# Gated delta rule, chunk stage: norms by ScalarE and TensorE, query rows four steps behind, offset products first

## The reference

```python
def _l2norm(x, eps=1e-06):
    return x * jax.lax.rsqrt(jnp.sum(x * x, axis=-1, keepdims=True) + eps)

def _gated_delta_rule(q, k, v, g, beta):
    q = _l2norm(q) * SCALE
    k = _l2norm(k)
    ...
    def step(S, inp):
        q_t, k_t, v_t, g_t, b_t = inp
        S = S * jnp.exp(g_t)[..., None, None]
        mem = jnp.einsum('bhk,bhkv->bhv', k_t, S)
        delta = (v_t - mem) * b_t[..., None]
        S = S + jnp.einsum('bhk,bhv->bhkv', k_t, delta)
        o_t = jnp.einsum('bhk,bhkv->bhv', q_t, S)
        return (S, o_t)
```

## Time and profile before

| | us |
|---|---|
| median of 3 runs | 886.2 (884.87 to 888.82) |
| the profiled execution | 885.32 |
| its span, first to last instruction | 883.2 |

### The profile page before, as it was taken

How to read it: one execution, slowest core, us unless ns; L and a number is a source line. 1 busy time by engine, 2 the same in 40 slices (tenths; PEclk the granted TensorE clock), 3 DMA queues, 4 the chain that set the end, 5 groups by cost and what they waited for, 6 DMA issues and landing times.

```text
span 883.2 us, 11650 instructions
## 1 busy us (share of the span) xinstructions
PE 787.4 (89%) x4040; PEld 566.3 (64%) x4040; DVE 542.7 (61%) x1302; ACT 252.3 (29%) x402; POOL 210.1 (24%) x191
## 2 busy tenths in 40 slices
PE   5889999888999999998988499799885999999974
PEld 4322333576777777776446478578652899999963
DVE  4599993654444444446799998995478244333426
ACT  2456667332333343333540001221310100000000
POOL 3550000021222222220031000474001344444310
PEclk9989999987999999999999699899997999999995
DMA  9683000101111111140221003400011899999944
GB/s 297 167 195 74 2 3 5 51 19 36 36 53 36 53 36 53 36 144 1 84 96 36 0 1 92 122 1 1 1 48 34 319 340 342 336 350 344 341 138 155
DMA packets 38034, 98.85 MB, mean 112 GB/s; under 512 B 5262, under 2 KB 18118, under 8 KB 37030
## 3 DMA queue, kind: packets, MB, share of 16 engines
q1 hardware_dynamic: 33894, 87.91, 31.1%
q0 software_dynamic: 3648, 9.97, 3.1%
q10 hardware_dynamic: 448, 0.39, 0.2%
HBM read 85.35 MB, written 13.69 MB: 112 GB/s over the span
## 4 chain that ended last, share of the span: by engine, by line
PE 63%; DVE 28%; DMA 4%; ACT 2%; issue 2%; SPq 1%; POOL 0%; ACTq 0%; DVEq 0%; POOLq 0%
PE psum L1246 16%; PE psum L1513 9%; PE psum L1523 8%; PE psum L1257 7%; PE psum L1146 3%; DVE arena L2003 3%; PE psum L1135 3%; PE psum L1125 3%; DVE arena L2062 3%; DVE arena L2055 2%; DVE small L1674 2%; DVE arena L1915 2%; PE psum L1407 1%; PE psum L1325 1%; PE psum L1264 1%
## 5 line engine op out<-in xcount | busy, mean ns | idle before, releaser
L1246 PE MATMUL psum<-xr,wr 128*128 128x512 f32 x600 | 158.8, 415 | 1.1 <-DVE arena L1823 1.1
L1246 PEld LDWEIGHTS psum<-xr,wr 128*128 128x128 f32 x600 | 115.9, 194 | 25.4 <-issue 1.3
L666 POOL TENSOR_TENSOR wr<-ring,wr 128x512 fp32r<-128x512 f32 (+1 forms) x50 | 54.3, 1104 | 197.8 <-ACT wr L829 197.8
L1674 DVE TENSOR_REDUCE small<-psum 128x1 f32<-128x512 f32 x128 | 80.9, 684 | 9.2 <-PE psum L1125 8.5
L1513 PEld LDWEIGHTS psum<-arena 128*128 128x128 f32 x700 | 83.4, 191 | 3.4 <-issue 1.5
L1513 PE MATMUL psum<-arena 128*128 128x128 f32 x700 | 83.9, 274 | 1.1 <-ACT arena L1013 1.1
L1523 PE MATMUL psum<-arena 128*128 128x256 f32 x350 | 81.8, 379 | 1.9 <-DVE arena L2227 1.9
L2216 DVE TENSOR_SCALAR arena<-psum,arena 128x256 f32<-128x256 f32 x35 | 16.9, 484 | 101.4 <-PE psum L1523 101.4
L1786 DVE TENSOR_TENSOR hid<-hid,psum 128x512 f32<-128x512 f32 x50 | 34.4, 688 | 68.4 <-ACT hid L835 68.4
L1257 PE MATMUL psum<-hr,wr 128*128 128x512 f32 x300 | 76.1, 389 | 0.2 <-DVE hr L1761 0.2
L808 ACT ACTIVATE arena<-psum 128x1024 f32<-128x1024 f32 x64 | 63.0, 1023 | 27.1 <-PE psum L1135 26.3
(11 more groups left out here) (360 smaller groups left out, 1232.2 us busy)
## 6 DMA issues: line engine op xcount, KB each, us to landing
arena<-in_w1u SPq DMA_DIRECT2D x35, 642.5 KB
arena<-in_w1d SPq DMA_DIRECT2D x35, 640.0 KB
ring<-in_w SPq DMA_DIRECT2D x25, 384.0 KB, 3.0
part_scratch<-arena SPq DMA_DIRECT2D x12, 256.0 KB, 4.2
arena<-z_scratch SPq DMA_DIRECT2D x8, 384.0 KB, 6.5
arena<-part_scratch SPq DMA_DIRECT2D x9, 256.0 KB, 7.8
qkv_scratch<-arena SPq DMA_DIRECT2D x4, 512.0 KB, 2.8
arena<-qkv_scratch SPq DMA_DIRECT2D x4, 512.0 KB, 4.0
```

Source lines behind the costliest of these rows:

```text
L666: pool.tensor_tensor(wr0[:, k, LO, part], ring0[:, k, part], wr0[:, k, HI, part], ALU.subtract).then_inc(s["w0_lo"], 1)
L1246: ins = pe.matmul(bank[2 * b + m][:, :], wr0[:, k, w, lo:lo + P], xr[:, x, f, half(b)], start=(f == 0 and (w, x) == PARTS[0]), stop=(f == ...
L1674: dve.tensor_reduce(nm[:, g % 2, at16:at16 + 1], full("scores", n), AX, ALU.max, negate=True).then_inc(s["bank_free"], 1)
```

## The change

It is a rewrite of the stage's order on all engines, with the buffers laid out anew to allow it:

- ACT squares k and q (`root`), PE sums the squares with 8 identity matmuls each (`norm_sum`), ACT takes the root from PSUM. The POOL squares and the DVE sums are gone.
- The scaling of the keys and of the queries moves from POOL to DVE. POOL keeps the decays.
- The 12 matmuls that spread the modulation rows go from behind the v convolution to ahead of the layer's projections, in place of a row of 10 warming matmuls; their ACT copies go along.
- PE sums the key pairs ahead of the second half of the v convolution.
- The solve handles the queries four steps behind the keys; the last four query steps stand alone, with the `Xt` rows written between them.
- Query products come first after the solve. The offset product of a key dimension (16 columns) is split from the matrix product (8 columns) and runs three dimensions ahead. All eight output products come last.
- SP turns half of the queries ahead of the offsets, and the rest behind.
- PE sums units 6, 7 and 8, then gathers groups 2 and 3, each in one piece; before, group 2 stood between unit 6 and 7 and group 3 was gathered in two halves.

```diff
+            root(0, k2, "k_to")
             act.wait_ge(s["d_in"], 5)
             act.activation(g_(5), g_(5), ACT.Exp, scale=-1.0).then_inc(s["d_act"], 1)
-            for n in range(2):
-                act.wait_ge(s["d_in"], n + 6)
-                act.activation(g_(8 + n), g_(8 + n), ACT.Sqrt, bias=1e-6).then_inc(s["d_act"], 1)
...
+            root(1, q2, "q_to")
...
+            def norm_sum(n):
...
+                for d in range(DK):
+                    ins = pe.matmul(bank[n][:, 0:CT], ident[:, :], squares(n)[:, d * CT:(d + 1) * CT],
+                                    start=(d == 0), stop=(d == DK - 1))
+                ins.then_inc(s["pair_sum"], 1)
...
             for i in range(C - 1, 0, -1):
-                due = queried(i - 1)
+                p = i + 4 if i < C - 4 else 0
...
+            for k in range(3):
+                offset_product(k)
+            for k in range(DK):
...
+                if k + 3 < DK:
+                    offset_product(k + 3)
...
-                if u in (2, 4, 6):
+                if u in (2, 4):
                     pe.wait_ge(s["state_out"], u)
-                    gather(u // 2 - 1, 0, CC)
-                if u == 7:
-                    pe.wait_ge(s["state_out"], 7)
-                    gather(NCG - 1, 0, 8)
+                    gather(u // 2 - 1)
+            gather(2)
             pe.wait_ge(s["state_out"], len(UNITS))
-            gather(NCG - 1, 8, CC)
+            gather(3)
```

More of the change, by code:

```diff
@@ L581, in _ @@
                              n_dram.rearrange("(h g) (u x) -> u h g x", g=NCG, u=VG)[v]).then_inc(s["n_to"], 16)
[L582 to L589, removed]
+            queries_out((2, 3), "qB_rest")
             for i in range(0, NT, 2):
@@ L679, in _ @@
             ch.link(pool.memset(Di, 1.0))
[L681 to L684, removed]
+            pool.wait_ge(s["d_act"], 7)
             for i in range(1, C):
@@ L890, in _ @@
             norm_out(2)
+            act.wait_ge(s["mod_mm"], 4)
+            for n in range(3):
+                act.activation(rows_mod[:, 4 * n:4 * n + 4, :], bank[4 + n].rearrange("p (m d) -> p m d", d=P),
+                               ACT.Copy).then_inc(s["g_silu"], 1)
             act.wait_ge(s["pads"], 1)
@@ L932, in _ @@
                     ins.then_inc(s["conv_silu"], 1)
+            for n in range(B):
+                conv_silu_v(n)
             for n in range(2 * B):
@@ L935, in _ @@
                 act.activation(yT[:, n // B, half(n % B)], bank[2 + n][:, :], ACT.Silu).then_inc(s["g_silu"], 1)
[L936 to L945, removed]
+            for n in range(B, 2 * B):
+                conv_silu_v(n)
             for x in range(2):
-                act.wait_ge(s["n_sum"], DK + x + 1)
+                act.wait_ge(s["n_sum"], x + 1)
                 act.activation(Qp.rearrange("p (x c t) -> p t x c", x=DK, c=CC)[:, 4 * x:4 * x + 4],
@@ L1307, in _ @@
             back(1)
-            for b in range(B):
-                warm(10, 7)
-                norm_tr(2, b)
+            pe.wait_ge(s["ones"], 5)
+            for m in range(12):
+                ins = pe.matmul(bank[4 + m // 4][:, tile(m % 4)], rows_col[:, m, :], ident[:, :],
+                                start=True, stop=True)
+            ins.then_inc(s["mod_mm"], 1)
+            norm_tr(2, 0)
+            warm(10, 7)
+            norm_tr(2, 1)
             pe.wait_ge(s["ld_sel"], 64)
@@ L1974, in _, with key_group @@
+            def key_group(x):
+                return slice(C + 4 * x, C + 4 * x + 4)
+            solved = [max(l_hi, ends)] * 2
+            asked = 0
             for i in range(C - 1, 0, -1):
-                due = queried(i - 1)
+                p = i + 4 if i < C - 4 else 0
                 prods = []
-                groups = [(slice(C, C + 4), 0), (slice(C + 4, 2 * C), 512), (slice(i, C), 1024)]
-                for x, (part, lo) in enumerate(groups):
+                if p:
+                    asked = max(asked, queried(p))
+                for x in range(2):
@@ L1987, in _ @@
+            ch.need(max(x_rows, asked, *solved))
             dve.memset(Sall[:, 0:VV * DK], 0.0).then_inc(s["blocks"], 1)
```

319 lines of the change are left out of this document (175 added, 144 removed).

## The result

The changed kernel takes **877.9 us**, the median of 4 runs (877.17 to 878.09). The kernel before took 887.5 in the runs made beside it (4 runs, 884.87 to 889.15). The ratio is 0.9875, with a 95% interval of 0.9846 to 0.9904 (it is estimated apart from the medians, whose quotient is 0.9892): faster, by 1.0 to 1.5%. The forecast was 876.0, in a range of 870 to 881.5, so it held. In a later series of five rounds the same kernel gave 877.22 against 888.03, ratio 0.9899 (0.9852 to 0.9945).

The account below looks back on a forecast made before the run. Three terms bound it: DVE to the solve's end (-3.7), what ends last before the scan's first sum (-2.2), PE behind the scan (-4.1). Together -10.0 from 885.3 gives 875.3, with 0.9 for the median 876.0 us; range 870 to 881.5.

Parts of the forecast that it names:

- The decays: POOL's seven small decay instructions fall beside DVE's multiplies, each holding one up for its own length: +2.2 us.
- the norms: DVE's sums over squares move to PE, so the reciprocal of the key norms comes earlier: -4.9 us.
- the cold PE: After the solve, idle PE restarts at a low clock; DVE waits 2.9 us for the first offset sum.
- Ahead of the norms: Spreading matmuls replace warming while DVE normalises; taken as 0, at most +0.5 us.
- POOL's two scalings: Leaving POOL, they no longer stretch two DVE pair multiplies: -4.2 us.
- rival 1: Cheaper than forecast: decays slip between DVE's multiplies (-2.2) or PE is not late (-2.9); down to 871 us, chance 0.15.
- The solve's bubbles: Eight or so steps of the last four query rows depend on their forerunner, 0.13 us each: +0.9 us.
- The turning: Turned offsets, ready 54.6 us after the solve's end, stay hidden before the scan, by 1.0 us only.
- rival 2: Ahead of the scan, the turning or PE stays last: 881 us, chance 0.13.
- The tail: Behind the scan, PE loses one row of gathers (3.6 us) and a 0.5 us wait: -4.1 us.
- Rival 3: Behind the scan, unit 8 waits for POOL and DVE, so 4.1 us does not come: 880 us, chance 0.08.
- Rival 4: PE's clock stays low over the scan's start, the scan waits 7 us, the end takes 14 more: 896 us, chance 0.03.

Follow-up runs that it names:

- e2_pool_scales: Changed kernel with the key and query scalings back on POOL; from layer 1's first DVE scaling to the solve's end 84.47 us instead of 82.42.
- e7_query_beside: Changed kernel with queries solved beside the keys again, Xt rows behind; from layer 1's first DVE scaling to the solve's end 86.21 us, 3.8 more.
- e4_warm_pe: Changed kernel with 54 dummy matmuls on PE during DVE's solve; from the solve's end to the scan's first sum 53.65 us instead of 56.64.
- e5_turn_late: Changed kernel with offsets sent to DRAM only once the block matrices are done; solve's end to scan's first sum 56.98 us instead of 56.64.
- e1_tail_old: Changed kernel with the old order of gathers put back; scan's first sum to the first transpose behind the scan 69.92 us instead of 65.20.
- e8_before_tail_new: Kernel before with only the new order of gathers; scan's first sum to the first transpose behind the scan 65.38 us, 3.9 shorter.
- e3_decays_early: Changed kernel with ACT's exponential for the decays ahead of the key root; layer 1's first DVE scaling to the solve's end 81.59 us, 0.83 less.

## Why the forecast held, step by step

The total of the changed part was forecast at -10.0 and came at -10.1, but that closeness is luck: terms that were off cancelled. The decays were 1.4 cheaper, the norms 0.5 dearer and the stretch behind the solve 1.0 dearer, most of it by the cold PE.

- **Ahead of the norms (0, measured 0).** The spreading matmuls take 2.84 us, and PE's projections end 35.8 us behind g in both kernels.
- **The norms (-4.9, measured -4.4).** The mechanism held: PE's projections ended, the norm sum stood next, and DVE waited for ACT. The path was mis-sized by 0.5 us: PE's 16 instructions took 1.95 instead of 1.8, and from their end to the reciprocal, by way of ACT's root, it took 0.88, where I had allowed 0.55. The squares cost nothing: ACT's square of k took 1.04 us and the table load behind it 1.28, and both were over at 447.98, ahead of PE's norm sum at 448.54.

```profile
448.54 1.95 PE L1353 MATMUL psum<-arena,ident 128*128 128x128 f32 x16
```

```profile
450.53 0.39 ACT L931 ACTIVATE rt<-psum 128x128 f32<-128x128 f32 x1 [2.54 <-PE psum L1353]
```

- **POOL's two scalings (-4.2) and their return to DVE (+2.3).** Both right. The query products, which no decay meets, fell by 2.17 us, the two scalings take 2.28 together, and e2_pool_scales gives 2.0 back.
- **The decays (+2.2, measured +0.8): the step that failed.** I took the two full stalls of the earlier trace rows as the pattern and charged DVE the whole length of each decay. For POOL's large scalings the pattern held again in e2_pool_scales: a multiply of 896 columns took 3,255 ns there against 1,087. For the decays it did not: five of DVE's multiplies lengthened by 87 to 220 ns, 30 to 52% of what each decay takes alone, and two decays cost next to nothing. This part of rival 1 came true.
- **The solve's bubbles (+0.9, measured +0.7).** Eight steps at 0.13, the forecast's own numbers, make 1.0 and not 0.9. The waits for PE that were held to be hidden, by 3 us or more, were hidden: DVE asked for the upper query pair sums 4.1 us and for the lower ones 2.7 us after PE had them; e7_query_beside shows the 4.3 us that the old order would have met.
- **The cold PE (a wait of 2.9, measured 3.7).** The mechanism was right, as e4_warm_pe shows by taking 3.0 of it away. The size was not: the query sums ended at T + 13.2, not 12.3. I had taken the loss of one earlier cold start for a constant. (The forecast's own terms, an offset sum at 15.9 and DVE ready at 13.2, make 2.7 and not 2.9.) Seven profiles have it between 2.3 and 3.7, so 2.9 lies in the middle of what the kernel does, and the profile of the changed kernel, twice, was at its upper end. This is most of the 1.0 that the second stretch lacks.
- **The turning (cover forecast 1.0, measured 2.0).** The turned offsets were ready at T + 54.6, just as forecast; the cover grew because DVE waited longer, and rival 2 did not come. e5_turn_late prices the turning's early start at 1.65.
- **The tail (-4.1, measured -4.1).** One row of gathers is gone (3.5 us, by the distance of the rows' starts), and so is the wait of 0.47, and all copies lie beside other work: 3.9 together, and the scan ahead of them is 0.2 shorter. Rival 3 did not come; e1_tail_old and e8_before_tail_new show the term from both sides. The 32 weight loads of a gather, which the forecast named as its pace, took 3.76 us for the 128 columns of group 2 in the kernel before, and 3.65 for each half of group 3, of 64.
- **Rival 4, the clock low over the scan's start.** It did not come. The clock was back at 1.00 by 503, more than half of PE's late output sums ran beside the scan's start, at a granted 1.00 in every window of 2 us from 551 to 561, and the scan's stretch lost nothing. A short low stretch of the clock later in the scan, as e1_tail_old met it, cost 0.76 there. The row is that of the last output sums, 72 in 16.2 us as the forecast had them:

```profile
544.99 16.24 PE L1393 MATMUL psum<-arena,ident 128*128 128x256 f32 x72
```

- **The total (875.3 for the profile, measured 877.75).** The +2.4 is not in the change: layer 0 was 3.4 longer in this profile, and the end 0.6 shorter. The forecast took the single profile of the kernel before for its layer 0 and left no room for that layer's scatter, which one trace does not show. By the same 3.4 us the scan's first sum stands at 551.81, past the 551 that the forecast named as a sign of being wrong; counted from g it lies at 548.4 of the old profile's time, where 548.5 was forecast.

What stays open: why the end of layer 0 moves by up to 7 us from run to run, and why the cold start is mild in one run and long in the next. No edit tried either.

## What to carry to other kernels

When an engine's work is moved off its path, ask what the others do in the idle time that the move makes or needs: here the new order could win 4.2 us between the solve and the scan (57.83 to 53.65), a PE left idle for 13 us gave 3.0 of them back, and dummy matmuls beside DVE's solve recovered them. A POOL instruction beside DVE's multiplies was dear where it was large (2.2 us for 1,024 columns) and cheap where it was small (0.8 us for seven of 16 to 112 columns), so large ones go to DVE and small ones may stay. And compare kernels by stretches between marks of the same work: here g to T repeats to 0.05 us over five profiles with the same code in it (82.40 to 82.45), where totals scatter by 1%. Look for what still moves inside a stretch: the cold start's wait moved one of them by 1.4 us.

## What was unexpected about the hardware

**Small POOL instructions hold DVE for less than their own length.** Groups by form in the changed kernel: a DVE multiply that meets a decay, and the same size without one.

```profile
L1935 DVE TENSOR_TENSOR arena<-hid,arena 128x896 f32<-128x896 f32 x1 | 1.2, 1174 | 0.0
L1935 DVE TENSOR_TENSOR hT<-hid,xn 128x896 f32<-128x896 f32 x1 | 1.1, 1087 | 0.0
...
L1935 DVE TENSOR_TENSOR arena<-hid,arena 128x512 f32<-128x512 f32 x1 | 0.9, 872 | 0.0
...
L1935 DVE TENSOR_TENSOR arena<-hid,xn 128x512 f32<-128x512 f32 x1 | 0.7, 684 | 0.0
```

For 896, 768, 640, 512 and 384 columns DVE lost 87, 119, 149, 188 and 220 ns. Laid over each other, these multiplies met the decays of 48, 64, 80, 96 and 112 columns: 1.8 to 2.0 ns for each column of POOL's. The decays alone took 222 ns for 16 columns and 426 for 112 in e3_decays_early, so 2.1 for a column and some 0.19 us that are there for any size. The decays of 16 and 32 columns met the two dependent products ahead and cost 0.03 us together. It looks as if only the part that grows with the columns keeps DVE out. That is an estimate from these rows; it was not tried by itself, and the two smallest decays cost even less. POOL fared worse: each decay took about as long as the DVE instruction that it met (1,262 ns beside one of 1,224, and 254 alone):

```profile
L695 POOL TENSOR_TENSOR arena<-arena,rt 128x32 f32<-128x32 f32 x1 | 1.3, 1262 | 0.1
...
L695 POOL TENSOR_TENSOR arena<-arena,rt 128x112 f32<-128x112 f32 x1 | 0.8, 751 | 0.1
```

**The cold start is not a constant.** After 13.07 us of idling PE was granted 0.50 in the changed kernel, and it reached 1.00 about 6 us after it resumed (it resumed at 495.57, and the window of 501 to 503 shows 0.83). In e1_tail_old, with the same code and the same idle time of 13.07 us, it was there some 3 us after PE resumed: the window of 498 to 500 already has 0.94. DVE's wait was 1.4 us shorter for it (timeline and window of PE in e1_tail_old):

```profile
495.09 0.76 PE L1400 MATMUL psum<-xn,ident 128*128 128x128 f32 x2 [13.07 <-DVE arena L2040]
```

```profile
498.00:500.00 2.00, 2.00 (x18) 0.94 0.00 0
```
